# The down projection's low rank products as narrow fp32 matmuls

## The chip, the cores and the metric

One core of one Trainium2 chip runs the whole program. The metric is the device time of one execution in microseconds; for the kernel before it is the median of three runs.

## The reference

Eight samples of 128 tokens, 512 features each. A gated feed forward network whose three projections each have a low rank addition chosen per sample by an index, then a second gated network with an RMS norm, then a residual. Cut to what matters:

```python
def lora_add(base, inp, A, B):
    Ab = A[layer_idx][lora_indices]          # [8, 16, F]: one matrix per sample
    Bb = B[layer_idx][lora_indices]
    t = jnp.einsum('bri,bni->bnr', Ab, inp)
    return base + jnp.einsum('bor,bnr->bno', Bb, t) * SCALE
gate = lora_add(jnp.einsum('bnh,fh->bnf', x, W_gate), x, A_gate, B_gate)
up = lora_add(jnp.einsum('bnh,fh->bnf', x, W_up), x, A_up, B_up)
act = jax.nn.silu(gate) * up
down = lora_add(jnp.einsum('bnf,hf->bnh', act, W_down), act, A_down, B_down)
```

Here F is 1376, the rank 16 and SCALE 0.5. The change concerns the `t` of the last line: for every sample, 16 rows of its own A against its own 128 tokens, summed over F.

## The kernel before, in words

Tokens lie in the free dimension, in two halves t = 0, 1 of 512 tokens (four samples each); features lie on the 128 partitions. F is 11 tiles of 128 (FC), the last one padded. All arithmetic on TensorE aims at fp32 accuracy by splitting: a value is rounded to the type `fp32r` (the hi part, a copy on ScalarE) and what is left is another `fp32r` value (the lo part, a subtraction on VectorE); a product takes three matmuls (`PASSES`: hi x hi, hi x lo, lo x hi). One PSUM bank holds 128 partitions by 512 fp32 values, which is one output tile of one half.

The program is five instruction streams written out by hand, one for each of TensorE (`pe`), VectorE (`v`), ScalarE (`a`), GpSimd (`pool`) and SyncE's DMA queue (`sp`), each in its own fixed order, tied by semaphores. No planner orders anything: the order in the source is the order on the engine.

The work runs in stages. First come the gate and up projections (first a few tiles on their own, then eight groups in a scheme with seven products each, `group(j)`, line 1421), which leave the activations `act` in SBUF as plain fp32. Then the **first down projection**, the stage of the change (lines 1526 to 1635). Its parts on TensorE are:

- `main_c(t, n)` (line 1532, matmuls on line 1528): activation tile n of half t against the weight tile `wdc[n]`, 4 output tiles by 3 passes, 12 matmuls of 512 columns. Its activation comes from a ring of ten slots (`slot_c`), filled by `hi_ac` on ScalarE and `lo_ac` on VectorE; `s_alo` counts filled slots, `s_use` counts used ones. Its weights come by DMA (`load_wd`), are split by `hi_wd` and `lo_wd`, and are counted by `s_wdlo`. A group of 11 for half 0 and of 11 for half 1.
- `t_c(t, n, ...)` (line 1538): the low rank product of this stage. `ad[:, n, t, :]` holds 128 weight columns: 4 samples by 16 of hi, then 4 by 16 of lo. Two matmuls of 512 columns (with the hi and the lo activation slot) give all four samples' A against all four samples' tokens. It runs between the `main_c` calls, since it reads the same slots.
- ScalarE's `td_add` moves the lower 64 rows of the result (the lo part of A) to SBUF; VectorE's `td_sum` adds them to the upper 64 rows and multiplies by a mask that holds 0.5 for the sample's own 16 rows and zero elsewhere; `td_hi` and `td_lo` split the sum into `td`.
- `lora_c(t, h)` (line 1545): B against `td`, two matmuls of 256 columns onto each output tile, which closes it.
- `p4(S1 - 1)` is the last product of the stage before, put between the first two `main_c`. `sum_squares` (line 1552) sums squares of the result over the features for the RMS norm, whose chain (`keep_y`, `square`, `sum_hi`, `rsqrt`, `norm`, `scale`) leads to the next stage's operands.

After the last `lora_c` of half 1 (`close(3)`) the second network begins with `conv` (line 1446).

Of the kernel before, what the change touches and what calls it, by code (L numbers as in the profile page):

```python
# [15 lines left out]
P = 128  # L16
KT = H // P
FC, FF = 11, 14
CH = 512
# [24 lines left out]
def build(nc, xT_in, idx_in, wsh_in, w0_in, wgu_in, wd_in, vs_in, vj_in, agu_in, bgu_in, ad_in, bd_in, lnw_in, out):  # L44
# [4 lines left out]
    with ctx:  # L49
# [21 lines left out]
        with ExitStack() as way:  # L71
            tadd = sb("tadd", [64, CH], f32, way)
            tsum = sb("tsum", [64, CH], f32, way)
            bdr = sb("bdr", [64, 2, H], f32, way)
# [54 lines left out]
        T_BANK = [bank[7], bank[1]]  # L129
# [73 lines left out]
        def unit_act(n):  # L203
# [35 lines left out]
        s_adhi, s_adlo, s_bdhi, s_bdlo = sem("ad_hi"), sem("ad_lo"), sem("bd_hi"), sem("bd_lo")  # L239
        s_ahi, s_alo, s_use = sem("act_hi"), sem("act_lo"), sem("act_used")  # L240
        s_t, s_tadd, s_tsum, s_tmsk, s_tdhi, s_tdlo = (sem(n) for n in (
            "td_projected", "td_added", "td_summed", "td_masked", "td_hi", "td_lo"))
# [131 lines left out]
        @block.gpsimd  # L374
        def _(pool):
            m = mask[0:64, :].rearrange("p (b n) -> p b n", b=4)
            nc.gpsimd.memset(mask[0:64, :], LORA_SCALE).then_inc(s_mask, 1)
            pool.wait_ge(s_mask, 1)
            nc.gpsimd.affine_select(out=m, in_=m, compare_op=ALU.is_ge, fill=0.0, base=0,
                                    pattern=[[-RANK, 4], [0, P]], channel_multiplier=1).then_inc(s_mask, 1)  # L380
            pool.wait_ge(s_mask, 2)
            nc.gpsimd.affine_select(out=m, in_=m, compare_op=ALU.is_ge, fill=0.0, base=RANK - 1,
                                    pattern=[[RANK, 4], [0, P]], channel_multiplier=-1).then_inc(s_mask, 1)
            pool.wait_ge(s_w0hi0, 2)
            nc.gpsimd.memset(act[CR:P, FC - 1, :], 0.0).then_inc(s_act_pad, 1)
            nc.gpsimd.memset(v32(tgu[KS:P, :, :, :]), 0.0).then_inc(s_pad, 1)
            nc.gpsimd.memset(v32(stk0[KS:P, :, :]), 0.0).then_inc(s_pad, 1)
            nc.gpsimd.memset(v32(stk1[KS:P, :, :]), 0.0).then_inc(s_pad, 1)
            nc.gpsimd.memset(v32(tneg[KS:P, :, :]), 0.0).then_inc(s_pad, 1)
            pool.wait_ge(s_p4, S1)  # L390
            for t in range(2):
                nc.gpsimd.memset(v32(bd[t][KS:P, :, :]), 0.0).then_inc(s_pad_d, 1)
                nc.gpsimd.memset(v32(td[t][KS:P, :]), 0.0).then_inc(s_pad_d, 1)

        @block.scalar
        def _(a):
# [200 lines left out]
            def hi_ad():  # L597
                a.wait_ge(s_ad_ld, 16 * B)
                a.wait_ge(s_stklo, 8)
                for b in range(B):  # L600
                    col = RANK * (b % 4)
                    copy(ad[:, :, b // 4, col:col + RANK], ad_raw[:, b, :].rearrange("p (n r) -> p n r", r=RANK)
                         ).then_inc(s_adhi, 1)
# [9 lines left out]
            def td_add(t):  # L613
                a.wait_ge(s_t, t + 1)
                for q in range(2):
                    half = slice(256 * q, 256 * q + 256)
                    copy(tadd[32 * q:32 * q + 32, half], T_BANK[t][64 + 32 * q:96 + 32 * q, half]).then_inc(s_tadd, 1)

            def td_hi(t):
                a.wait_ge(s_tmsk, 2 * t + 2)  # L620
                copy(td[t][0:32, :], tsum[0:32, :]).then_inc(s_tdhi, 1)
                copy(td[t][32:64, :], tsum[0:32, :]).then_inc(s_tdhi, 1)
# [132 lines left out]
            for j in range(S1):  # L755
                group(j, S1)
                if j < 6:
                    stack_hi(j // 2 + 2, j % 2)
                elif j == 6:
                    hi_ad()  # L760
# [10 lines left out]
            td_add(0)  # L771
            td_hi(0)
# [16 lines left out]
            td_add(1)  # L789
            td_hi(1)  # L790
# [55 lines left out]
        def _(v):  # L846
# [163 lines left out]
            def lo_ad():  # L1010
                for b in range(B):
                    col = RANK * (b % 4)
                    v.wait_ge(s_adhi, b + 1)
                    sub(ad[:, :, b // 4, 64 + col:64 + col + RANK], ad_raw[:, b, :].rearrange("p (n r) -> p n r", r=RANK),
                        ad[:, :, b // 4, col:col + RANK]).then_inc(s_adlo, 1)

# [6 lines left out]
            def td_sum(t):  # L1023
                v.wait_ge(s_tadd, 2 * t + 2)
                if t == 1:
                    v.wait_ge(s_tdhi, 2)
                    v.wait_ge(s_tdlo, 1)
                for q in range(2):
                    rows, half = slice(32 * q, 32 * q + 32), slice(256 * q, 256 * q + 256)
                    nc.vector.tensor_tensor(tadd[rows, half], tadd[rows, half], T_BANK[t][rows, half], ALU.add  # L1030
                                            ).then_inc(s_tsum, 1)
                for q in range(2):
                    rows, half = slice(32 * q, 32 * q + 32), slice(256 * q, 256 * q + 256)
                    v.wait_ge(s_tsum, 2 * t + q + 1)
                    nc.vector.tensor_tensor(tsum[0:32, half], tadd[rows, half], mask[rows, half], ALU.mult
                                            ).then_inc(s_tmsk, 1)

            def td_lo(t):
                v.wait_ge(s_tdhi, 2 * t + 1)
                v.wait_ge(s_tmsk, 2 * t + 2)  # L1040
                sub(td[t][64:KS, :], tsum[0:32, :], td[t][0:32, :]).then_inc(s_tdlo, 1)
# [166 lines left out]
            for j in range(S1):  # L1208
                group(j, 0, S1)
                if j == 6:  # L1210
                    lo_ad()
# [14 lines left out]
            td_sum(0)  # L1226
            td_lo(0)
# [17 lines left out]
            td_sum(1)  # L1245
            td_lo(1)
# [84 lines left out]
        def _(pe):  # L1331
# [227 lines left out]
            pe.wait_ge(s_adlo, B)  # L1559
# [19 lines left out]
            pe.wait_ge(s_c21[1], S1 // 2)  # L1579
            pe.wait_ge(s_c12, S1)  # L1580
            pe.wait_ge(s_alo, 12)
            main_c(1, 0, range(3))
            pe.wait_ge(s_tadd, 2)
            pe.wait_ge(s_tsum, 2)
            main_c(1, 0, range(3, 4))
            pe.wait_ge(s_alo, 13)
            main_c(1, 1)
# [4 lines left out]
            pe.wait_ge(s_tdhi, 2)  # L1592
            pe.wait_ge(s_tdlo, 1)
            main_c(0, 10)
            for h in range(4):
                lora_c(0, h).then_inc(s_y, 1)
            pe.wait_ge(s_alo, 14)
            main_c(1, 2).then_inc(s_use, 1)
            pe.wait_ge(s_alo, 15)
            main_c(1, 3)  # L1600
            pe.wait_ge(s_ev, 2)
            t_c(1, 0, True, False).then_inc(s_use, 1)
            for n in range(1, 4):
                t_c(1, n, False, False)
            pe.wait_ge(s_alo, 16)
            main_c(1, 4)
            t_c(1, 4, False, False)
            sum_squares(0, 0)
            for n in range(5, 7):
                pe.wait_ge(s_alo, 11 + n + 1)  # L1610
                main_c(1, n)
                t_c(1, n, False, False)
            for n in range(7, 11):
                pe.wait_ge(s_alo, 11 + n + 1)
                ins = t_c(1, n, False, n == 10)
            ins.then_inc(s_t, 1)
# [12 lines left out]
            pe.wait_ge(s_tdhi, 4)  # L1629
            pe.wait_ge(s_tdlo, 2)  # L1630
# [15 lines left out]
            pe.wait_ge(s_tsum, 4)  # L1646
# [112 lines left out]
```

## Time and profile before

| what | value |
|---|---|
| median of 3 runs | 410.06 us (408.87 to 410.11) |
| the profiled execution's own time | 411.35 us |
| span of its core, first to last instruction | 409.5 us |
| granted TensorE clock, mean | 1.000 |
| instructions | 5437, of them 1849 matmuls |

The span is the profiled part of that execution; its own time is what the runs' times are to be compared with. PE is TensorE's matmul row, PEld its weight load row, DVE is VectorE, ACT is ScalarE, POOL is GpSimd. Matmul records overlap, so that 390 ns of one record don't say how far apart two of them start. Line numbers are those of the kernel before; `L848` and `L398` are helpers (a subtraction on DVE, a copy on ACT), so there the names of the tiles tell which step it is.

### The profile page before, as it was taken

How to read it: one execution, taken by the hardware profiler on the slowest of the kernel's cores; microseconds unless marked ns; L12 is line 12 of the kernel's file. 1: busy time of each engine (PE TensorE's matmuls, PEld its weight loads, DVE VectorE, ACT ScalarE, POOL GpSimd, SP SyncE). 2: the span in 40 equal slices, each digit the busy share in tenths (PEclk: the TensorE clock that was granted, in tenths of full speed). 3: DMA queues.
4: the chain of work that ended last, by engine and by line, in shares of the span. 5: the costliest groups of instructions: out<-in, count | busy, mean ns of one | idle time of the engine just before them, and what ended most of it. 6: DMA issues, size and time to landing. Idle time of an engine off the chain costs nothing.

```text
span 409.5 us, 5437 instructions
## 1 busy us (share of the span) xinstructions
PE 403.8 (99%) x1849; PEld 336.0 (82%) x1849; DVE 314.1 (77%) x483; ACT 239.8 (59%) x377; POOL 12.7 (3%) x16
## 2 busy tenths in 40 slices
PE   8999999999999999999999999999999999999996
PEld 5899888888888888888888888888888888888885
DVE  3779979585856567463889988778787869899993
ACT  4759876757674467731655555555656476384740
POOL 5300000000000200000000000000000000000000
PEclk9999999999999999999999999999999999999999
DMA  7630233311111420300101113131322125205112
GB/s 252 201 113 2 78 108 108 114 51 53 51 53 53 128 78 0 104 0 0 49 4 40 64 52 102 53 102 52 103 84 72 51 90 155 89 1 194 52 51 102
DMA packets 14237, 31.86 MB, mean 78 GB/s; under 512 B 2307, under 2 KB 4611, under 8 KB 14211
## 3 DMA queue, kind: packets, MB, share of 16 engines
q1 hardware_dynamic: 13632, 29.96, 22.6%
q10 hardware_dynamic: 578, 1.57, 1.2%
q8 instruction: 14, 0.23, 0.2%
q14 instruction: 13, 0.10, 0.1%
HBM read 29.43 MB, written 2.10 MB: 77 GB/s over the span
## 4 chain that ended last, share of the span: by engine, by line
PE 97%; DMA 1%; issue 0%; DVE 0%; DVEq 0%; SPq 0%
PE bank L1337 47%; PE bank L1663 16%; PE bank L1528 15%; PE bank L1446 5%; PE bank L1474 3%; PE bank L1493 3%; PE bank L1482 3%; PE bank L1541 2%; PE bank L1347 2%; DMA wraw<-w_in 1%; PE bank L1548 0%; PE bank L1555 0%; DVE act L930 0%; DVEq L49 0%; SPq L289 0%
## 5 line engine op out<-in xcount | busy, mean ns | idle before, releaser
L1337 PE MATMUL bank<-xs,ws 128*128 128x512 f32 x840 | 194.2, 390 | 0.0
L1337 PEld LDWEIGHTS bank<-xs,ws 128*128 128x128 f32 x840 | 156.6, 188 | 32.3 <-ACT bank L398 0.5
L1528 PE MATMUL bank<-xs,wdc 128*128 128x512 f32 x264 | 62.9, 389 | 0.0
L1528 PEld LDWEIGHTS bank<-xs,wdc 128*128 128x128 f32 x264 | 49.3, 188 | 10.1
L398 ACT ACTIVATE xs<-act 128x512 fp32r<-128x512 f32 x71 | 43.0, 625 | 21.1 <-DVE act L995 7.6
L848 DVE TENSOR_TENSOR xs<-act,xs 128x512 fp32r<-128x512 f32 x71 | 47.6, 686 | 4.7 <-ACT xs L398 4.2
L848 DVE TENSOR_TENSOR ws<-wraw,ws 128x256 fp32r<-128x256 f32 (+2 forms) x49 | 32.4, 670 | 14.9 <-ACT ws L398 14.9
L398 ACT ACTIVATE bank<-bank 128x512 f32<-128x512 f32 x30 | 17.4, 580 | 39.5 <-PE bank L1337 38.7
L1663 PE MATMUL bank<-xs,vs 128*128 128x512 f32 x168 | 38.2, 389 | 0.0
L1663 PEld LDWEIGHTS bank<-xs,vs 128*128 128x128 f32 x168 | 31.5, 188 | 6.5
L398 ACT ACTIVATE ws<-wraw 128x256 fp32r<-128x256 f32 (+2 forms) x47 | 28.6, 619 | 12.0 <-PE bank L1337 4.1
L848 DVE TENSOR_TENSOR ws<-wsum,ws 128x1024 fp32r<-128x1024 f32 x20 | 24.5, 1225 | 12.4 <-ACT ws L398 12.4
L398 ACT ACTIVATE mu<-bank 128x512 f32<-128x512 f32 x40 | 23.9, 598 | 17.2 <-PE bank L1337 10.6
L1663 PE MATMUL bank<-xs,ws 128*128 128x512 f32 x126 | 29.0, 389 | 0.0
L1663 PEld LDWEIGHTS bank<-xs,ws 128*128 128x128 f32 x126 | 23.6, 188 | 4.9
L398 ACT ACTIVATE stack<-bgu_raw 32x1024 fp32r<-32x1024 f32 (+1 forms) x20 | 22.8, 1138 | 0.3
L467 ACT ACTIVATE act<-bank 128x512 f32<-128x512 f32 (+1 forms) x30 | 17.4, 593 | 9.4 <-PE bank L1347 8.0
L1446 PE MATMUL bank<-xs,ws 128*128 128x512 f32 x96 | 22.1, 389 | 0.0
L398 ACT ACTIVATE ws<-wsum 128x1024 fp32r<-128x1024 f32 x20 | 21.1, 1053 | 0.8 <-DVE wsum L862 0.8
L1446 PEld LDWEIGHTS bank<-xs,ws 128*128 128x128 f32 x96 | 18.0, 188 | 3.7
L848 DVE TENSOR_TENSOR wdc<-wdr,wdc 128x512 fp32r<-128x512 f32 x11 | 7.6, 688 | 12.6 <-ACT wdc L398 12.6
L848 DVE TENSOR_TENSOR stack<-bgu_raw,stack 32x1024 fp32r<-32x1024 f32 (+1 forms) x10 | 13.2, 1322 | 2.4 <-ACT stack L398 2.2
(124 smaller groups left out, 438.6 us busy)
## 6 DMA issues: line engine op xcount, KB each, us to landing
wraw<-wgu_in SPq DMA_DIRECT2D x22, 512.0 KB, 3.2
wdr<-vs_in SPq DMA_DIRECT2D x7, 512.0 KB, 3.5
wdr<-wd_in SPq DMA_DIRECT2D x11, 256.0 KB, 2.7
wraw<-vj_in SPq DMA_DIRECT2D x3, 896.0 KB, 4.6
xa<-xT_in SPq DMA_DIRECT2D x4, 256.0 KB, 5.0
wraw<-w_in SPq DMA_DIRECT2D x4, 256.0 KB, 5.2
xa<-xT_in ACTq DMA_DIRECT2D x2, 512.0 KB, 5.9
bgu_raw<-bgu_in SPq DMA_DIRECT2D x32, 32.0 KB, 2.0
```

The source lines that it names most:

```text
L398: return nc.scalar.activation(out_ap, in_ap, ACT.Copy, scale=scale)
L467: return nc.scalar.activation(out_ap, in_ap, ACT.Silu, scale=scale)
L848: return nc.vector.tensor_tensor(out_ap, raw, v32(part), ALU.subtract)
L1337: ins = mm(z[:, :], ws[:, j % 2, w, s, k * P:(k + 1) * P], xs[:, c, r, k, :], start=(start and k == 0 and s == 0 and r == 0), stop=(k == 1 ...
L1347: ins = mm(z[0:m, half], stk[c % 2][:, 2 * t + q, cols], t_op[:, half], start=(alone and q == 0), stop=(q == 1), skip_group_check=True)
L1446: ins = mm(z[:, :], ws[:, j % 2, w, s, (k % 2) * P:(k % 2) * P + P], x_op(k, t, r), start=(k == 0 and s == 0 and r == 0), stop=(k == KT - ...
L1474: mm(UNIT_BANK[i][g][:, :], w0_tile(s, k, g, i), x_op(k, 0, r), start=(k == 0 and s == 0 and r == 0), stop=(k == KT - 1 and r == 1), skip_ ...
L1482: mm(UNIT_BANK[n][g][:, :], w0_tile(s, k, g, UNITS[n][0]), x_op(k, 1, r), start=(k == 0 and s == 0 and r == 0), stop=(k == KT - 1 and s == ...
L1493: ins = mm(SHORT_BANK[t][g][:, half], wsh[s][:, k, g, q, :], x_op(k, t, r)[:, half], start=(k == 0 and s == 0 and r == 0 and q == 0), stop ...
L1528: ins = mm(z[:, :], wd[:, s, h * P:(h + 1) * P], x[r], start=(start and s == 0 and r == 0), stop=False, skip_group_check=True)
L1541: ins = mm(T_BANK[t][:, :], ad[:, n, t, :], slot_c(u, r), start=(first and r == 0), stop=(last and r == 1), skip_group_check=True)
L1663: ins = mm(DOWN[p][3][h][:, :], down_w(i, s)[:, h * P:(h + 1) * P], slot_f(i, r), start=(p < 2 and k == 0 and s == 0 and r == 0), stop=(k ...
```

## The change

The low rank products of the first down projection are no longer made of hi and lo parts. `ad` becomes plain fp32, with 48 columns for each pair of samples and each tile n: the even sample's 16, 16 zeros (set by GpSimd), the odd sample's 16. A window of 32 columns is then one sample's A with 16 zeros behind or ahead of it. Each product takes such a window and that sample's 128 tokens of `act`, both plain fp32, and writes 32 partitions of the bank, 32b to 32b + 31 for the sample b of the half: 44 products for a half. Both halves run one after the other, right behind `main_c(0, 3)`, instead of spread over the stage. ScalarE reads the four samples' blocks out of the bank with the factor 0.5 (`td_scale`), which needs neither mask nor addition, and `td_hi` and `td_lo` follow for both halves ahead of the last weight tile. Half 1's bank is bank 6 instead of bank 1. The ring's slots are now free after `main_c`, so `s_use` is counted there, and `main_c(1, n)` runs without a break.

```diff
-            ad = sb("ad", [P, FC, 2, P], f32r, way)
+            ad = sb("ad", [P, B // 2, FC, 3 * RANK], f32, way)
-        T_BANK = [bank[7], bank[1]]
+        T_BANK = [bank[7], bank[6]]
...
             nc.gpsimd.memset(v32(tneg[KS:P, :, :]), 0.0).then_inc(s_pad, 1)
+            pool.wait_ge(s_stklo, 8)
+            nc.gpsimd.memset(ad[:, :, :, RANK:2 * RANK], 0.0).then_inc(s_ad_pad, 1)
+            pool.wait_ge(s_ad_pad, 1)
             pool.wait_ge(s_p4, S1)
...
-            def td_add(t):
+            def td_scale(t):
                 a.wait_ge(s_t, t + 1)
-                for q in range(2):
-                    half = slice(256 * q, 256 * q + 256)
-                    copy(tadd[32 * q:32 * q + 32, half], T_BANK[t][64 + 32 * q:96 + 32 * q, half]).then_inc(s_tadd, 1)
+                for b in range(4):
+                    copy(tsum[:, t, b * P:(b + 1) * P], T_BANK[t][32 * b:32 * b + 32, b * P:(b + 1) * P], LORA_SCALE
+                         ).then_inc(s_tsum, 1)
...
+            for t in range(2):
+                td_scale(t)
+                td_hi(t)
             hi_wd(FC - 1)
             hi_ac(10)
             hi_bd()
             for u in range(11, 18):
                 hi_ac(u)
-            td_add(0)
-            td_hi(0)
             nc.scalar.preload_act_table(ACT.Abs_reciprocal_sqrt)
...
             rsqrt(0)
-            td_add(1)
-            td_hi(1)
...
             for n in range(2, FC - 1):
                 lo_wd(n)
                 lo_ac(n)
+            td_lo(0)
+            td_lo(1)
             lo_wd(FC - 1)
...
             for u in range(11, 18):
                 lo_ac(u)
-            td_sum(0)
-            td_lo(0)
...
             v.wait_ge(s_lnws, 1)
-            td_sum(1)
-            td_lo(1)
...
-            def t_c(t, n, first, last):
-                u = 11 * t + n
-                for r in range(2):
-                    ins = mm(T_BANK[t][:, :], ad[:, n, t, :], slot_c(u, r),
-                             start=(first and r == 0), stop=(last and r == 1), skip_group_check=True)
+            def t_c(t):
+                for n in range(FC):
+                    for b in range(4):
+                        tokens, col = slice(b * P, (b + 1) * P), RANK * (b % 2)
+                        ins = mm(T_BANK[t][32 * b:32 * b + 32, tokens], ad[:, 2 * t + b // 2, n, col:col + 2 * RANK],
+                                 act_at(ORDER_C[n], t)[:, tokens], start=(n == 0), stop=(n == FC - 1), skip_group_check=True)
                 return ins
...
-            pe.wait_ge(s_adlo, B)
...
+                main_c(0, n).then_inc(s_use, 1)
                 if n == 0:
-                    main_c(0, 0)
                     p4(S1 - 1)
-                    pe.wait_ge(s_b22, S1)
-                    t_c(0, 0, True, False).then_inc(s_use, 1)
-                elif n < 9:
-                    main_c(0, n)
-                    t_c(0, n, False, False).then_inc(s_use, 1)
-                else:
-                    t_c(0, 9, False, False)
-                    pe.wait_ge(s_alo, 11)
-                    t_c(0, 10, False, True).then_inc(s_t, 1)
-                    main_c(0, 9).then_inc(s_use, 1)
...
+                if n == 3:
+                    pe.wait_ge(s_ad, B)
+                    pe.wait_ge(s_ad_pad, 1)
+                    pe.wait_ge(s_cl, S1)
+                    pe.wait_ge(s_shm, 2)
+                    pe.wait_ge(s_act_pad, 1)
+                    pe.wait_ge(s_um, 4)
+                    pe.wait_ge(s_c21[1], S1 // 2)
+                    t_c(0).then_inc(s_t, 1)
+                    pe.wait_ge(s_c12, S1)
+                    pe.wait_ge(s_c12f, S1 // 2)
+                    pe.wait_ge(s_c22f, S1 // 2)
+                    t_c(1).then_inc(s_t, 1)
+            pe.wait_ge(s_alo, 11)
             pe.wait_ge(s_wdlo, FC)
+            main_c(0, 10).then_inc(s_use, 1)
...
+            pe.wait_ge(s_tdhi, 4)
+            pe.wait_ge(s_tdlo, 2)
             for h in range(4):
                 lora_c(0, h).then_inc(s_y, 1)
...
+            pe.wait_ge(s_tsum, 8)
+            for n in range(7):
                 pe.wait_ge(s_alo, 11 + n + 1)
-                main_c(1, n)
-                t_c(1, n, False, False)
...
+                ins = main_c(1, n)
+                if n == 0:
+                    ins.then_inc(s_use, 1)
+                elif n == 3:
+                    sum_squares(0, 0)
+            pe.wait_ge(s_alo, 22)
```

`lo_ad`, `td_sum`, `tadd` and the 128 column form of `ad` are gone; `hi_ad` becomes `place_ad`, which makes the same eight copies into the new form.

## Rows read from the trace of the kernel before

**Rows 1.** The page's busy line of TensorE and its chain of waits, by engine.
```profile
PE 403.8 (99%) x1849; PEld 336.0 (82%) x1849; DVE 314.1 (77%) x483; ACT 239.8 (59%) x377; POOL 12.7 (3%) x16
...
PE 97%; DMA 1%; issue 0%; DVE 0%; DVEq 0%; SPq 0%
```

**Rows 2.** The stretches view: stretch, its length, each engine's busy us, PEclk, DMA.
```profile
core 0: us, PE busy (x) PEld busy (x) DVE busy (x) ACT busy (x) POOL busy (x), PEclk, DMA share, GB/s
...
128.03:201.97 73.94, 73.94 (x336) 61.46 (x334) 45.23 (x72) 38.73 (x65) 2.79 (x4) 1.00 0.15 47
```

**Rows 3.** The chain in order of time, 126 to 206 us: start us, us, what.
```profile
132.51 0.47 PE bank L1541 x2
...
135.71 0.45 PE bank L1541 x2
136.16 2.72 PE bank L1528 x12
...
157.92 1.36 PE bank L1541 x6
...
170.16 0.95 PE bank L1548 x8
...
176.58 1.81 PE bank L1541 x8
...
181.12 0.46 PE bank L1541 x2
...
184.82 0.45 PE bank L1541 x2
...
188.00 2.27 PE bank L1541 x10
```

**Rows 4.** TensorE's groups by line, 128.03 to 201.97 us: count, busy us, mean ns.
```profile
L1541 PE MATMUL bank<-xs,ad 128*128 128x512 f32 x44 | 12.1, 390 | 0.0
L1548 PE MATMUL bank<-ws 128*128 128x256 f32 x16 | 2.7, 281 | 0.0
```

**Rows 5.** TensorE's matmuls and weight loads in order of time, around one t_c.
```profile
138.27 0.62 PE L1528 MATMUL bank<-xs,wdc 128*128 128x512 f32 x2
138.50 0.41 PEld L1541 LDWEIGHTS bank<-xs,ad 128*128 128x128 f32 x2
138.72 0.61 PE L1541 MATMUL bank<-xs,ad 128*128 128x512 f32 x2
138.95 2.68 PEld L1528 LDWEIGHTS bank<-xs,wdc 128*128 128x128 f32 x12
```

**Rows 6.** VectorE, then GpSimd, in order of time: start us, us, what, idle before.
```profile
132.55 0.69 DVE L914 SCALAR_TENSOR_TENSOR act<-bank,act 128x512 f32<-128x512 f32 x1 [1.57 <-PE bank L1347]
...
133.76 0.68 DVE L848 TENSOR_TENSOR xs<-act,xs 128x512 fp32r<-128x512 f32 x1
...
177.86 0.69 DVE L848 TENSOR_TENSOR xs<-sqr,xs 128x512 fp32r<-128x512 f32 x1 [0.70 <-ACT xs L398]
...
132.57 0.95 POOL L392 MEMSET ws<- 32x1024 f32 x1 [118.44 <-PE bank L1347]
133.47 0.52 POOL L393 MEMSET ws<- 32x512 f32 x1
```

**Rows 7.** ScalarE in order of time, then two of its groups by line.
```profile
150.35 0.64 ACT L398 ACTIVATE wdc<-wdr 128x512 fp32r<-128x512 f32 x1
...
159.52 0.78 ACT L398 ACTIVATE tadd<-bank 32x256 f32<-32x256 f32 x2
162.39 1.29 ACT L398 ACTIVATE ws<-tsum 32x512 fp32r<-32x512 f32 x2 [2.09 <-DVE tsum L1035]
...
166.05 2.18 ACT L398 ACTIVATE ws<-wraw 128x768 fp32r<-128x768 f32 x4
170.43 2.07 ACT L398 ACTIVATE nx<-bank 128x512 f32<-128x512 f32 x4 [2.21 <-PE bank L1548]
...
L398 ACT ACTIVATE ws<-tsum 32x512 fp32r<-32x512 f32 x4 | 2.5, 632 | 4.1 <-DVE tsum L1035 4.0
...
L398 ACT ACTIVATE tadd<-bank 32x256 f32<-32x256 f32 x4 | 1.5, 379 | 7.6 <-PE bank L1541 7.5
```

More of the change, by code:

```diff
@@ L71, in build @@
         with ExitStack() as way:
-            tadd = sb("tadd", [64, CH], f32, way)
-            tsum = sb("tsum", [64, CH], f32, way)
+            tsum = sb("tsum", [32, 2, CH], f32, way)
             bdr = sb("bdr", [64, 2, H], f32, way)
@@ L238, in build @@
         s_wdhi, s_wdlo = sem("wd_hi"), sem("wd_lo")
-        s_adhi, s_adlo, s_bdhi, s_bdlo = sem("ad_hi"), sem("ad_lo"), sem("bd_hi"), sem("bd_lo")
+        s_ad, s_ad_pad, s_bdhi, s_bdlo = sem("ad_placed"), sem("ad_padding_zero"), sem("bd_hi"), sem("bd_lo")
         s_ahi, s_alo, s_use = sem("act_hi"), sem("act_lo"), sem("act_used")
-        s_t, s_tadd, s_tsum, s_tmsk, s_tdhi, s_tdlo = (sem(n) for n in (
-            "td_projected", "td_added", "td_summed", "td_masked", "td_hi", "td_lo"))
+        s_t, s_tsum, s_tdhi, s_tdlo = (sem(n) for n in ("td_projected", "td_scaled", "td_hi", "td_lo"))
         s_y, s_sq, s_sqd, s_acc, s_sqhi, s_sqlo, s_ev, s_nm = (sem(n) for n in (
@@ L595, in copy_u2, with place_ad @@
                     copy(du2[:, i, :], DB_BANK[i][:, :]).then_inc(s_dcu, 1)
-            def hi_ad():
+            def place_ad():
                 a.wait_ge(s_ad_ld, 16 * B)
@@ L600, in hi_ad @@
                 for b in range(B):
-                    col = RANK * (b % 4)
-                    copy(ad[:, :, b // 4, col:col + RANK], ad_raw[:, b, :].rearrange("p (n r) -> p n r", r=RANK)
-                         ).then_inc(s_adhi, 1)
+                    col = 2 * RANK * (b % 2)
+                    copy(ad[:, b // 2, :, col:col + RANK], ad_raw[:, b, :].rearrange("p (n r) -> p n r", r=RANK)
+                         ).then_inc(s_ad, 1)
             def hi_bd():
@@ L611, in hi_bd @@
                     copy(bd[t][64:KS, :, :], raw).then_inc(s_bdhi, 1)
-            def td_add(t):
+            def td_scale(t):
                 a.wait_ge(s_t, t + 1)
-                for q in range(2):
-                    half = slice(256 * q, 256 * q + 256)
-                    copy(tadd[32 * q:32 * q + 32, half], T_BANK[t][64 + 32 * q:96 + 32 * q, half]).then_inc(s_tadd, 1)
+                for b in range(4):
+                    copy(tsum[:, t, b * P:(b + 1) * P], T_BANK[t][32 * b:32 * b + 32, b * P:(b + 1) * P], LORA_SCALE
+                         ).then_inc(s_tsum, 1)
             def td_hi(t):
-                a.wait_ge(s_tmsk, 2 * t + 2)
-                copy(td[t][0:32, :], tsum[0:32, :]).then_inc(s_tdhi, 1)
-                copy(td[t][32:64, :], tsum[0:32, :]).then_inc(s_tdhi, 1)
+                a.wait_ge(s_tsum, 4 * t + 4)
+                copy(td[t][0:32, :], tsum[:, t, :]).then_inc(s_tdhi, 1)
+                copy(td[t][32:64, :], tsum[:, t, :]).then_inc(s_tdhi, 1)
             def keep_y(m):
@@ L759, in _ @@
                 elif j == 6:
-                    hi_ad()
+                    place_ad()
             for n in range(FC - 1):
@@ L1008, in lo_ac @@
                 sub(slot_c(u, 1), act_at(ORDER_C[n], t), slot_c(u, 0)).then_inc(s_alo, 1)
[L1010 to L1015, printed above, removed]
             def lo_bd():
@@ L1021, in lo_bd @@
                         ).then_inc(s_bdlo, 1)
[L1023 to L1036, printed above, removed]
             def td_lo(t):
                 v.wait_ge(s_tdhi, 2 * t + 1)
-                v.wait_ge(s_tmsk, 2 * t + 2)
-                sub(td[t][64:KS, :], tsum[0:32, :], td[t][0:32, :]).then_inc(s_tdlo, 1)
+                v.wait_ge(s_tsum, 4 * t + 4)
+                sub(td[t][64:KS, :], tsum[:, t, :], td[t][0:32, :]).then_inc(s_tdlo, 1)
             def add_square(t, h):
@@ L1209, in _ @@
                 group(j, 0, S1)
-                if j == 6:
-                    lo_ad()
             c22_sum(S1 - 1)
@@ L1565, in _ @@
                 pe.wait_ge(s_wdlo, n + 1)
+                main_c(0, n).then_inc(s_use, 1)
                 if n == 0:
-                    main_c(0, 0)
                     p4(S1 - 1)
-                    pe.wait_ge(s_b22, S1)
-                    t_c(0, 0, True, False).then_inc(s_use, 1)
-                elif n < 9:
-                    main_c(0, n)
-                    t_c(0, n, False, False).then_inc(s_use, 1)
-                else:
-                    t_c(0, 9, False, False)
-                    pe.wait_ge(s_alo, 11)
-                    t_c(0, 10, False, True).then_inc(s_t, 1)
-                    main_c(0, 9).then_inc(s_use, 1)
[L1579 to L1587, printed above, removed]
+                if n == 3:
[12 more added lines that the diff above has]
+            pe.wait_ge(s_alo, 11)
             pe.wait_ge(s_wdlo, FC)
+            main_c(0, 10).then_inc(s_use, 1)
             pe.wait_ge(s_bdhi, 4)
@@ L1591, in _ @@
             pe.wait_ge(s_pad_d, 4)
-            pe.wait_ge(s_tdhi, 2)
-            pe.wait_ge(s_tdlo, 1)
-            main_c(0, 10)
+            pe.wait_ge(s_tdhi, 4)
+            pe.wait_ge(s_tdlo, 2)
             for h in range(4):
                 lora_c(0, h).then_inc(s_y, 1)
[L1597 to L1603, printed above, removed]
-                t_c(1, n, False, False)
[L1605 to L1609, printed above, removed]
-                pe.wait_ge(s_alo, 11 + n + 1)
-                main_c(1, n)
[L1612 to L1616, printed above, removed]
+            pe.wait_ge(s_tsum, 8)
+            for n in range(7):
+                pe.wait_ge(s_alo, 11 + n + 1)
+                ins = main_c(1, n)
[4 more added lines that the diff above has]
+            pe.wait_ge(s_alo, 22)
             def rest(h):
@@ L1628, in _ @@
             rest(2)
-            pe.wait_ge(s_tdhi, 4)
-            pe.wait_ge(s_tdlo, 2)
             close(0)
```

1 line of the change is left out of this document (removed).

## The prediction

> **What bounds the kernel now.** I read the page's busy line first, then its chain of waits, then the stretches, then the chain in order of time. TensorE is busy 99% of the span with 1,849 matmuls, and 97% of the chain that ends last is TensorE itself [rows 1]. In the stretch that the change rewrites, 128.03 to 201.97 us, it never rests: 73.94 of 73.94 us busy at a granted clock of 1.00, which is the 2.4 GHz level, while VectorE is busy 45.23 and ScalarE 38.73 us [rows 2]. So a matmul taken out is worth its own step, and VectorE or ScalarE work taken out is worth nothing unless TensorE waits for it. The step is read from the chain in order of time: twelve matmuls of 512 columns take 2.72 us, 0.2267 us each; eight of 256 columns take 0.95 us, 0.119 us each [rows 3]. A single record lasts 390 ns or 281 ns [rows 4]; it overlaps the next, so the chain's step is the price.
>
> **What is removed.** t_c had 44 matmuls of 512 columns [rows 4]. In the chain they stand as one pair of 0.47 us, seven of 0.45 us, runs of 1.36, 1.81 and 2.27 us, and pairs of 0.46 and 0.45 us [rows 3]: 0.47 + 3.15 + 1.36 + 1.81 + 0.46 + 0.45 + 2.27 = 9.97 us, all on the path. The rest of line 1528's matmuls, p4, lora_c and sum_squares stay, in another order.
>
> VectorE loses lo_ad and td_sum, ScalarE td_add, and PE the waits for them. I price these at 0: TensorE did not wait for any of them [rows 2].
>
> **What is added on TensorE.** 88 products of 32 weight columns by 128 tokens, plain fp32, in two runs of 44 after the fourth main_c. No row shows an fp32 product or one narrower than 128 weight columns, so both ends come from the nearest rows. The two steps lie on a line, (0.2267 - 0.119) / 256 per column, which puts 128 columns at about 0.065 us, an estimate. Cheapest: one pass each and four at a time, 22 x 0.065 = 1.4 us. Dearest: an fp32 value is, in this kernel, a rounded part and a remainder; their products make four combinations, so 4 x 128 = 512 columns, the 0.2267 us row, and each product alone in its turn: 88 x 0.2267 = 19.9 us. Between them lies four combinations with four products at a time: 22 x 0.2267 = 5.0 us. I take 5.0. For the width: the steps of 512 and 256 columns follow the columns that stream, though each has a full load of 128 weight columns of its own; that load is hidden, since the 188 ns load of the next matmul starts while the one before is in flight [rows 5]. For four at a time: the four samples of a group write four different quarters of the bank's partitions, so they need no common columns of the array. Nothing in the trace shows the array used so; that is the open point, and the rivals are made of it. Entering and leaving the narrow shape may cost one emptying of the array each: 0.390 - 0.227 = 0.16 us, twice, 0.3 us.
>
> The Trainium skill, TensorEngine Tiling (Array Packing), Key Properties, says that column tiles run independently and that a change of the tiling mode drains TensorE; no run here shows either. The Trainium skill, FP8 and Floating Point Precision, TensorE Precision Notes, gives true FP32 four passes; the Trainium skill, Perfetto Trace Analysis, Engine Utilization, only halves the output rate for FP32_LOW_HIGH, by which the sum would have 2.6 us in place of 5.0.
>
> **What is moved, and what might wait.** Without t_c the PE clock reads: main_c(0,1) begins at 132.5, main_c(0,3) ends at 140.7, the two runs end at 146.0 (with 5.3 us), main_c(0,9) ends at 162.3, lora_c at 166.0, the fourth main_c of the second half at 176.8.
> - Weights and activations of the first groups: the remainder of slot 2 is done at 134.4 [rows 6]; PE now needs it at 135.2 instead of 136.2 [rows 3]. The margin shrinks to 0.8 us and grows again by the length of the runs. Nothing.
> - The runs' inputs: the last activation is multiplied at 132.55 to 133.24 [rows 6], 7 us before 140.7. POOL's memset of ad (704 values a partition, between the 0.5 us of 512 values and the 0.95 us of 1,024) lies in a stretch where POOL is idle for 118 us [rows 6]; its later memsets wait for p4 as before, so nothing queued behind it is late. DVE's next waits are for weights. The moved PE waits cost nothing.
> - ScalarE now has td_scale and td_hi for both halves ahead of hi_wd(10), which starts at 150.35 before [rows 7]. Eight copies of 32x128 are at most eight of the 379 ns copies of 32x256 [rows 7], say 0.29 us; with four of 632 ns [rows 7] this is 4.9 us, in place of the 4.17 us (with its wait) from 159.52 to 163.69 [rows 7]. Everything up to keep_y is thereby 0.7 us late: hi_wd(10) at 155.3, hi_bd done at 160.7, bd's remainder some 1.2 us later. PE wants slot 10 at 162.3 and bd at 165.0: covered. lo_wd(10) on DVE waits with it; SP's next loads wait for later work than that.
> - keep_y started at 170.43, right after lora_c. ScalarE is now free for it at 169.0 (end of hi_b at 168.23 [rows 7], plus 0.7), 3 us after lora_c's end; it becomes the late one. The square's remainder came 8.1 us after keep_y's start (178.55 [rows 6]), so at 177.1; sum_squares(0, 0) is reached at 176.8. A wait of 0.3 us. Beyond it, norm(0) no longer queues behind td_sum(1) on DVE and scale is some 9 us early: nothing.
> - Behind close(3) the order and the waits are those of before; SP and POOL have no issue moved past another.
>
> **Sum.** -9.97 + 5.0 + 0.3 + 0.3 = -4.4 us, on a span of 409.5 us. The profiled execution took 411.35 us in all, 1.3 us above the median of 410.06, so the same difference on the median gives **405.7 us**, 1.1% faster. A measurement of this kernel can tell about 0.3%, 1.2 us, from no change.
>
> **Rivals.**
> 1. *Products in turn* (slower). The four quarters do not run together, or the array is held as one whatever the output's partitions say, so the change doesn't do what its shape promises. Price: 88 x 0.2267 = 19.9 us in place of 5.0, no wait at sum_squares: -9.97 + 19.9 + 0.3 = +10.2, so 420.3 us. It decides from 44 steps on: above 44 x 0.2267 = 9.97 us the runs cost more than what they replace. For it: no row shows two matmuls of this kernel sharing the array. Against it: loads and matmuls here do overlap [rows 5]. The Trainium skill, TensorE: Matmul & The Clock Gate, Part 3, has a rule that speaks for it: a load runs beside a matmul in flight only where the row groups differ, and these four share all 128 rows. By that rule the four would go one by one; the trace disagrees for the full array, where loads into the same rows start before the last matmul is done (188 ns loads within 227 ns steps) [rows 5].
> 2. *Half side by side* (same or slightly slower). An fp32 product goes as two records, one for the weights' rounded part and one for the remainder, each streaming 256 columns at 0.119 us. Both use the same quarter, and the records of this trace start in program order, so the second waits for the first, and only it overlaps the next product's first: 88 x 0.119 = 10.5 us, with 0.3 us 10.8, so +0.8: 410.9 us. With four records of 128 columns three of them are exposed: 88 x 3 x 0.065 = 17.2 us, +7.5: 417.6. For it: the kernel's own split needs two weight loads. Against it: an f32r product is one load and one matmul (1,849 of each) [rows 1].
> 3. *The wait takes it back.* If ScalarE's copies from the bank cost the full 379 ns and DVE's chain adds to that, sum_squares waits 1.5 us rather than 0.3: 406.9 us. It stays on the faster side, within my case.
>
> **How the numbers follow.** My case 0.46 (rival 3 is in it), half side by side 0.32, in turn 0.22. Faster by over 0.3%: my case and a sliver of rival 2, 0.47. Within 0.3%: rival 2 with two records and few extras, 0.13. Slower: the rest of rival 2 and all of rival 1, 0.40. My case's own range is 403.5 to 407.5: down if a product streams only as much as 256 columns (22 x 0.119 = 2.6 in place of 5.0), up for the wait and for groups that take 0.3 us. The whole range, 403.5 to 417.5, takes in rival 2 and leaves out rival 1. The bound of 1.4 us (402.1) has no reason of its own and is left out too.
>
> **What would show it.** In the profile after: two runs of line t_c near 140.7 us that last about 5 us together, four starts close to one another and then a gap of some 0.22 us; main_c(0,4) at about 146; sum_squares(0, 0) within 0.5 us of its turn; close(3) near 197.5 instead of 201.9, and all later work shifted by the same 4.4 us. Records twice or four times 88, evenly spaced, mean rival 2; even starts 0.2 us apart mean rival 1. A granted clock below 1.00 in the runs' stretch would make any of these prices too low, and the prediction wrong on the slow side.

## The result and the profile after

The changed kernel takes 405.18 us in the median of 4 runs (404.01 to 406.00), the kernel before, on the same chips, 409.47 us (408.69 to 410.11). The ratio is 0.9882, with a 95% interval from 0.9855 to 0.9910: 1.2% faster, where 1.1% and 405.7 us were forecast. The profiled execution took 405.77 us with a span of 403.9 us.

The page of the changed kernel, its busy line and its chain of waits by engine (they answer to [rows 1]):

```profile
PE 398.2 (99%) x1981; PEld 332.0 (82%) x1981; DVE 309.1 (77%) x467; ACT 240.5 (60%) x381; POOL 13.4 (3%) x17
...
PE 97%; DMA 1%; issue 0%; DVE 0%; DVEq 0%; SPq 0%
```

TensorE still sets the end, and it is as busy as before. With one matmul record for each of the 88 products it would have 88 - 44 = 44 records more; it has 1981 - 1849 = 132 = 176 - 44. So each of the 88 fp32 products is two matmul records on the chip, each with a weight load of its own. The stage's chain in order of time, 126 to 206 us (answers to [rows 3]; L1502 is main_c, L1516 t_c, L1523 lora_c, L1530 sum_squares, L1420 conv):

```profile
127.64 2.72 PE bank L1502 x12
130.36 1.36 PE bank L1311 x6
131.72 0.23 PE bank L1321 x2
131.95 8.19 PE bank L1502 x36
140.13 4.94 PE bank L1516 x176
145.08 19.31 PE bank L1502 x84
164.38 0.95 PE bank L1523 x8
165.34 10.91 PE bank L1502 x48
176.25 0.48 PE bank L1530 x2
176.73 15.01 PE bank L1502 x66
...
196.57 0.23 PE bank L1523 x2
196.80 2.07 PE bank L1420 x9
```

This is one unbroken row of TensorE work, with the run of narrow products as a single piece of 4.94 us. The same two ends in the kernel before, where L1528 is main_c and L1446 conv:

```profile
128.20 2.72 PE bank L1528 x12
...
202.13 2.07 PE bank L1446 x9
```

From the first main_c to the first conv it is 196.80 - 127.64 = 69.16 us, where the kernel before took 202.13 - 128.20 = 73.93 us: 4.77 us less. That covers the whole change of the median (4.3 us) and most of that between the two profiled spans (409.5 to 403.9, 5.6 us). The other 0.8 us lies where the code of TensorE is the same: 0.56 us ahead of the stage, 0.27 us behind it. In the kernels below main_c(0,0) starts anywhere between 125.7 and 127.9 us, so this part is a difference of executions, not of the change.

TensorE's groups by line in that stretch, and the narrow loads (answers to [rows 4]):

```profile
L1516 PE MATMUL bank<-act,ad 128*32 128x128 f32 x176 | 5.0, 273 | 0.0
...
L1516 PEld LDWEIGHTS bank<-act,ad 128*32 128x32 f32 x176 | 4.7, 110 | 0.4 <-issue 0.4
```

A record of 273 ns every 4.94 / 176 = 28 ns: by the modelled ends, some ten are in flight at a time. What the groups hide are the starts. Taken from the trace's records, they come four at a time; the numbers are nanoseconds from one start to the next, at the run's start and in its middle, with the wide matmuls' own step (227) ahead:

```
wide, wide, then the run:  227 227 318   7   6   7 113   7   7   6  90   6   7   7  89 ...
middle of the run:         ...  89   6   7   7  89   7   6   7  89 ...
the run's end, then wide:  ...  89   7   7   6 203 341 240 235
```

Four records start within 20 ns, then 89 ns pass: 109.5 ns for four. 44 such groups are 4.82 us. Going in costs 318 - 227 = 91 ns, coming out 203 - 89 = 114 ns at the first wide start and 341 - 227 = 114 ns at the second, 0.32 us in all for the way in and out.

### The profile page after: what moved, and what is told of

The parts are those of the page before. It is cut to its first block, busy times and chain, and to the rows that moved or that the text cites. A ratio compares the mean times of both kernels' runs of the same rounds, so it can differ in the third digit from the quotient of the medians.

```text
span 403.9 us, 5691 instructions
## 1 busy us (share of the span) xinstructions
PE 398.2 (99%) x1981; PEld 332.0 (82%) x1981; DVE 309.1 (77%) x467; ACT 240.5 (60%) x381; POOL 13.4 (3%) x17
## 4 chain that ended last, share of the span: by engine, by line
PE 97%; DMA 1%; issue 0%; DVE 0%; DVEq 0%; SPq 0%
PE bank L1311 47%; PE bank L1618 17%; PE bank L1502 15%; PE bank L1420 5%; PE bank L1448 3%; PE bank L1467 3%; PE bank L1456 3%; PE bank L1321 2%; PE bank L1516 1%; DMA wraw<-w_in 1%; PE bank L1523 0%; PE bank L1530 0%; DVE act L930 0%; DVEq L49 0%; SPq L287 0%
## 5 line engine op out<-in xcount | busy, mean ns | idle before, releaser
L1502 PE MATMUL bank<-xs,wdc 128*128 128x512 f32 x264 | 61.5, 390 | 0.0
L1502 PEld LDWEIGHTS bank<-xs,wdc 128*128 128x128 f32 x264 | 49.1, 188 | 10.2 <-DVE xs L848 0.2
L1420 PE MATMUL bank<-xs,ws 128*128 128x512 f32 x96 | 22.1, 389 | 0.0
L399 ACT ACTIVATE ws<-wsum 128x1024 fp32r<-128x1024 f32 x20 | 21.1, 1054 | 0.8 <-DVE wsum L862 0.8
L1420 PEld LDWEIGHTS bank<-xs,ws 128*128 128x128 f32 x96 | 18.0, 188 | 3.7
```

Of the source, the lines that this page charges most:

```text
L399: return nc.scalar.activation(out_ap, in_ap, ACT.Copy, scale=scale)
L1420: ins = mm(z[:, :], ws[:, j % 2, w, s, (k % 2) * P:(k % 2) * P + P], x_op(k, t, r), start=(k == 0 and s == 0 and r == 0), stop=(k == KT - ...
L1502: ins = mm(z[:, :], wd[:, s, h * P:(h + 1) * P], x[r], start=(start and s == 0 and r == 0), stop=False, skip_group_check=True)
```

## The experiments

Nine kernels, all made from the changed one. Each alters either t_c's loops or the place of the run; what the low rank product computes is the reference's, except where the expectation says otherwise. The times are medians; the ratio to the kernel before comes from runs of both on the same chip. The kernel before had 409.4 to 411.0 us in these series.

**1. The samples in turn.**

```diff
-                for n in range(FC):
-                    for b in range(4):
+                for b in range(4):
+                    for n in range(FC):
```

> The same 88 products, but all eleven tiles of one sample before the next sample, so that neighbours use the same quarter of the array. Theory SIDE (what the four quarters do at the same time is what makes the run short, and one record of 128 fp32 columns streams for about 0.1095 us): 176 records one behind the other, 176 x 0.1095 = 19.3 us in place of 4.94, some 14.3 us more than the changed kernel's 405.2, so 419.5 us. Rival RECORD (a narrow record is cheap whichever quarter it uses, 28 ns each, because its weight load is short): the run stays at 4.9 us and the time at 405.2 us.

Measured: 415.43 us, ratio 1.0119 (1.0080 to 1.0157), 10.2 us above the changed kernel's median. The same 176 records, in the chain of this kernel:

```profile
138.54 16.49 PE bank L1516 x176
155.03 19.27 PE bank L1502 x84
```

RECORD falls: the same records with the same loads take 16.49 us in place of 4.94 when neighbours share a quarter. So what the changed kernel lives on is the four quarters streaming together. SIDE is right in kind, and its run is 2.8 us too long: within one sample the records do start 109 ns apart, but at each border between samples the starts read

```
109 109 110   5 104  30  79  30  79  30 109 109
```

Two rows of starts, 109 ns apart each, run through one another for some four records. No record names its quarter; two rows at the pace of one quarter each are read as the next sample's records starting while the last ones of the sample before still wait for theirs. Seven borders save 2.8 us, 0.4 us or 3.6 records each. So TensorE does not start narrow records strictly in program order, and the description ahead of the prediction, by which the order in the source is the order on the engine, does not hold for them.

**2. Two samples in alternation.**

```diff
-                for n in range(FC):
-                    for b in range(4):
+                for pair in range(2):
+                    for n, b in [(n, 2 * pair + i) for n in range(FC) for i in range(2)]:
```

> The same 88 products, two samples in alternation, then the other two. SIDE: two quarters at a time, 88 x 0.1095 = 9.6 us in place of 4.94, 4.7 us more: 409.9 us, the time of the kernel before. RECORD: 4.9 us, 405.2 us.

Measured: 408.30 us, ratio 0.9961 (0.9936 to 0.9985), and in the chain of this kernel

```profile
140.36 8.53 PE bank L1516 x176
```

With two quarters at a time the run takes 8.53 us. The 1.1 us that lack to the expected 9.6 are three borders of the kind above. SIDE holds.

**3. Half the columns.**

```diff
-                        tokens, col = slice(b * P, (b + 1) * P), RANK * (b % 2)
+                        tokens, col = slice(b * P, b * P + 64), RANK * (b % 2)
```

> Each product streams only the first 64 of its sample's 128 tokens; the other 64 are left out of the low rank product. SIDE, with the columns streamed as the price: 44 groups of four at 0.053 + 0.003 us = 2.5 us, 2.4 us less than the changed kernel: 402.8 us. RECORD, with weight loads or the issue of records as the price: 176 x 28 ns as before, 4.9 us, 405.2 us.

Measured: 404.88 us, ratio 0.9874 (0.9826 to 0.9923): not told apart from the changed kernel. By the median RECORD would win, but the chain of this kernel says otherwise:

```profile
138.31 2.58 PE bank L1516 x172
140.89 2.26 issue
143.15 0.30 PE bank L1516 x4
```

172 of the 176 records pass in 2.58 us, in groups of four that are 56 ns apart: 53 ns of streaming and 3 ns, as SIDE has it. Then TensorE stands for 2.26 us, put down to "issue", with no semaphore behind it, and the last four follow. The gain was made and lost within the run. Experiment 9 takes that gap up.

**4. Eight runs instead of one stretch.** Two or three groups of four products stand behind every three matmuls of main_c(0,4) and (0,5).

```diff
-                main_c(0, n).then_inc(s_use, 1)
+                if n in (4, 5):
+                    for h in range(4):
+                        ins = main_c(0, n, range(h, h + 1))
+                        for tile in range(3 * h, min(3 * h + 3, FC)):
+                            last = t_c(n - 4, range(tile, tile + 1))
+                        if h == 3:
+                            last.then_inc(s_t, 1)
+                else:
+                    ins = main_c(0, n)
+                ins.then_inc(s_use, 1)
...
-                    t_c(0).then_inc(s_t, 1)
...
-                    t_c(1).then_inc(s_t, 1)
```

> The same products in the same order, but in eight runs of eight or twelve, each behind three wide matmuls of the fifth and sixth weight tile, instead of in one unbroken stretch. If going in and out of the narrow shape empties the array (0.32 us for a run by the gaps in the trace of the changed kernel): 7 x 0.32 = 2.2 us more, 407.4 us. If the gaps belong to the run's start alone (weights to be fetched, first records): 405.2 us. ScalarE's reads come some 2 us later in either case, and sum_squares may wait up to 0.5 us.

Measured: 407.09 us, ratio 0.9914 (0.9887 to 0.9941), 1.9 us above the changed kernel. Its chain:

```profile
140.74 0.79 PE bank L1516 x24
141.53 0.89 PE bank L1502 x3
142.43 0.79 PE bank L1516 x24
```

24 records should take 6 x 0.1095 = 0.66 us and take 0.79; three wide matmuls should take 0.68 and take 0.89. Each round trip between the shapes costs 0.13 + 0.21 = 0.34 us. Seven more of them are 2.4 us, and from the first main_c to the first conv this kernel takes 199.14 - 127.56 = 71.58 us, 2.42 us more than the changed kernel; sum_squares does not wait. That agrees with the emptying of 0.16 us each way that the prediction worked out. It is what the changed kernel saves by placing both runs together: with no other shape between them, they pay it once.

**5. Plain fp32 without the narrow shape.**

```diff
+                wide = ad[:, 2 * t:2 * t + 2, :, :].rearrange("p q n c -> p (q n c)")
                 for n in range(FC):
-                    for b in range(4):
-                        tokens, col = slice(b * P, (b + 1) * P), RANK * (b % 2)
-                        ins = mm(T_BANK[t][32 * b:32 * b + 32, tokens], ad[:, 2 * t + b // 2, n, col:col + 2 * RANK],
-                                 act_at(ORDER_C[n], t)[:, tokens], start=(n == 0), stop=(n == FC - 1), skip_group_check=True)
+                    ins = mm(T_BANK[t][:, :], wide[:, 32 * n:32 * n + P],
+                             act_at(ORDER_C[n], t), start=(n == 0), stop=(n == FC - 1), skip_group_check=True)
```

> Plain fp32 without the narrow shape: 22 products of 128 weight columns by all 512 tokens in the place of the 88. As weights each reads 128 neighbouring columns of the narrow form, so the low rank term that is added is another one than the reference's. The narrow run showed two records for each fp32 product, and 0.1095 us of streaming for one record of 128 columns. Theory FOUR (each of the two records streams every column twice): 22 x 2 x 0.43 = 18.9 us in place of 4.94, 14 us more than the changed kernel's 405.2: 419 us. Rival TWO (a wide fp32 product streams its columns twice in all): 9.4 us, 409.7 us.

Measured: 418.23 us, ratio 1.0225 (1.0208 to 1.0242). Its records and its chain:

```profile
L1515 PE MATMUL bank<-act,ad x44: 590/592/592, 138.1 to 156.5; 128*128 128x512 f32 x44
```

```profile
138.24 18.88 PE bank L1515 x44
```

FOUR holds: 44 records in 18.88 us, 429 ns each, which is twice the 213 ns that 512 columns take at 2.4 GHz, and 3 ns. With two records a product that makes four passes. The Trainium skill, FP8 and Floating Point Precision, TensorE Precision Notes, gives four; the trace agrees. The halved rate that the Trainium skill, Perfetto Trace Analysis, Engine Utilization, gives for FP32_LOW_HIGH fits one record here; a sum by it alone is short by a factor of two, since a product is two records. Plain fp32 on the full array makes the kernel 2.2% slower: the type alone does not give the gain, the narrow shape is needed. The other half of that question, rounded parts in the narrow shape, was not run.

**6. Two tiles deep.**

```diff
-                for n in range(FC):
-                    for b in range(4):
+                for first in range(0, FC, 2):
+                    for b, n in [(b, n) for b in range(4) for n in range(first, min(first + 2, FC))]:
```

> The same 88 products with two tiles of one sample ahead of the next sample, so that four records of one quarter stand in a row in the program. Theory REACH (TensorE starts a record ahead of older ones whose quarter is busy, but only some four records ahead, as the borders between samples in the kernel with the samples in turn suggest): about two quarters at a time, 7 to 10 us in place of 4.94: 407.5 to 410 us. Rival FAR (it looks as far ahead as it needs): 5 us, 405.2 us. Rival ORDER (records start strictly in program order): three of four records of a quarter exposed, 88 x 3 / 4 x 2 x 0.1095 = 14.5 us, 414.7 us.

Measured: 404.64 us, ratio 0.9897 (0.9878 to 0.9915), and in the chain of this kernel

```profile
138.39 5.15 PE bank L1516 x176
```

ORDER falls, and REACH, as I had put it, falls too: with four records of a quarter in a row all four quarters still stream together. Twelve older records stood ahead of the fourth quarter's first one. A reach counted over the whole program can't be both about four (experiment 1) and above twelve. One counted for each quarter can, which made the next theory.

**7. The run five groups later.**

```diff
-                if n == 3:
+                if n == 8:
                     pe.wait_ge(s_ad, B)
```

> The two runs stand behind the ninth main_c of the first half instead of the fourth; nothing else changes. If only TensorE's own work counts: 405.2 us. By the theory that the run's place is covered by ScalarE only while its result is there when ScalarE comes to it (148.0 us in the changed kernel's trace): the results come at 153.3 and 155.7 us, ScalarE is then some 5 us late down to keep_y and the squares, the eleventh main_c waits 1 us for its slot and sum_squares(0, 0) some 3 us more: 408 to 410 us.

Measured: 414.02 us, ratio 1.0122 (1.0102 to 1.0141): 8.8 us above the changed kernel, more than the 3 to 5 that I worked out. The run itself takes 4.95 us (151.91 to 156.86 us). TensorE's waits in this kernel, 150 to 200 us, where the changed kernel has none:

```profile
PE bank L1530 <- DVE xs L848: 3.9, 1, 3.9
PE bank L1502 <- DVE xs L848: 1.7, 1, 1.7
PE bank L1523 <- ACT ws L399: 0.6, 1, 0.6
```

ScalarE stood 8.12 us for the products:

```profile
154.59 1.15 ACT L399 ACTIVATE tsum<-bank 32x128 f32<-32x128 f32 x4 [8.12 <-PE bank L1516]
```

It had all that it has to do for main_c(0,10), lora_c and the squares queued behind that. The places are those of the expectation (slot, then bd, then sum_squares); the sizes add up to 6.2 us. More came from the clock. The chain of this kernel behind the last wait, then its stretches around it (engine busy columns as in [rows 2]):

```profile
181.44 0.93 PE bank L1530 x2
182.37 16.40 PE bank L1502 x66
...
177.40:181.40 4.00, 0.18 (x1) 0.00 (x0) 2.70 (x5) 2.72 (x5) 0.00 (x0) 1.00 0.18 72
181.40:184.40 3.00, 2.96 (x8) 2.37 (x9) 2.90 (x7) 0.69 (x1) 0.00 (x0) 0.57 0.00 0
184.40:190.00 5.60, 5.60 (x25) 4.55 (x24) 5.50 (x8) 1.90 (x2) 0.00 (x0) 0.93 0.00 0
```

After TensorE had rested for 3.9 us, the granted clock fell to a mean of 0.57 for 3 us, most of the time at its lower level (1.2 GHz), and the 66 matmuls that take 15.01 us in the changed kernel took 16.40. The remaining 1.2 us I put down to the matmuls next to each wait, which overlap none on that side (sum_squares' two take 0.93 us in place of 0.48); that sum is not shown piece by piece.

**8. Four tiles deep.** As experiment 6 with 4 in the place of 2.

```diff
-                for n in range(FC):
-                    for b in range(4):
+                for first in range(0, FC, 4):
+                    for b, n in [(b, n) for b in range(4) for n in range(first, min(first + 4, FC))]:
```

> The same 88 products with four tiles of one sample ahead of the next sample: eight records of one quarter in a row. Theory QUEUE (records are handed out in program order, and each quarter holds about four of them, running one included; a full quarter holds up all that come behind): worked through with 0.1095 us a record and four places this gives 9.3 us, in place of 4.94 (the same working gives 16.2 for the samples in turn, 8.4 for the pairs and 4.9 for two deep, measured 16.5, 8.5 and 5.15): some 409.5 us. With three places 11.8 us, 412 us. Rival FAR (no bound that matters): 5 us, 405 us.

Measured: 409.84 us, ratio 0.9988 (0.9963 to 1.0013), and in the chain of this kernel

```profile
140.39 9.98 PE bank L1516 x176
```

QUEUE's four places gave 9.3 us, three 11.8, FAR 5. The run took 9.98, as long as the 44 matmuls that the change removed, and the time is that of the kernel before. Four places for each quarter thus give all five orders to within 0.7 us: 4.8, 4.9, 8.4, 9.3, 16.2 worked through against 4.94, 5.15, 8.53, 9.98, 16.49. Only the 9.3 was worked out ahead of its run; the other four were known when the theory was made. "About four places" is what the runs support; nothing in them shows a queue as such.

**9. Half the columns, the two runs apart.** As experiment 3, with the second half's run one main_c later.

```diff
                     t_c(0).then_inc(s_t, 1)
+                if n == 4:
                     pe.wait_ge(s_c12, S1)
```

> As with 64 tokens a product (the other 64 left out), but the second half's run stands one main_c later than the first half's. Theory SUPPLY (the gap of 2.26 us in the run of 64 columns is TensorE out of instructions, since the run takes 352 records in 2.6 us): 2.7 us of wide matmuls between let the supply catch up, the gap goes or shrinks below 1 us, at the price of one more entry of 0.3 us: 403.0 us. Rival FIXED (something else holds the run's end): a gap of 2 us stays: 405 us.

Measured: 404.17 us, ratio 0.9859 (0.9820 to 0.9897). TensorE in order of time in this kernel:

```profile
139.06 1.44 PE L1516 MATMUL bank<-act,ad 128*32 128x64 f32 x88
140.43 3.03 PE L1502 MATMUL bank<-xs,wdc 128*128 128x512 f32 x12
143.39 1.44 PE L1516 MATMUL bank<-act,ad 128*32 128x64 f32 x88
144.76 15.50 PE L1502 MATMUL bank<-xs,wdc 128*128 128x512 f32 x67
```

The gap is gone: each run of 88 records takes 1.4 us without a break. That speaks for SUPPLY, and against anything tied to the end of the products. The time did not follow all the way, since sum_squares now waits for the squares:

```profile
PE bank L1530 <- DVE xs L848: 0.9, 1, 0.9
```

So 404.2 stands where 403.0 was expected, and against 404.9 of experiment 3 the difference is no more than the executions scatter.

The traces' DMA records fit SUPPLY too. In experiment 3 one packet of 16 KB on an instruction queue runs from 140.34 to 141.67 us: it is still under way when the stop begins (140.89 us), and the last four records follow 1.5 us behind it. In the changed kernel the packet of this place (141.84 to 142.72 us) is through 2 us before the run's last four records start, in experiment 9 (140.83 to 141.71 us) nearly 3 us. No row says which engine that queue feeds, so that instructions ran out in experiment 3 remains an inference, from where the stop lies, from what removes it and from this packet.

## Why the prediction was right

**What bounds the kernel.** Right. In experiments 1, 2, 5, 6 and 8 only the order or shape inside the run differs, TensorE shows no wait in the stage, and the time follows the run's length: 1 + (run - 9.97) / 410 gives 1.016, 0.996, 1.022, 0.988 and 1.000 for measured 1.0119, 0.9961, 1.0225, 0.9897 and 0.9988. All but the first lie in the measured intervals, and that one lies just above its upper end (1.0157).

**What is removed, 9.97 us.** Experiment 8 confirms it by substitution: a run of 9.98 us gives the old time back, with lo_ad, td_sum and td_add still taken out. So that work was worth nothing measurable, as priced, though VectorE's busy time between the first main_c and the first conv fell from 45.06 to 42.03 us.

**What is added, 5.0 us.** 4.82 us measured. The mechanism was right, four passes and four products at a time: a group of four takes 2 x 0.1095 = 0.219 us, where 0.2267 was taken. The form was not foreseen. Each product is two records of 0.1095 us, not one of 0.2267, so four starts are followed by a gap of 0.09 us and not of 0.22. I had taken pairs of records for the mark of the half-overlapped rival, at 10.5 us or more, since the second would hold up all that follows. The pairs were there, in groups of four rather than evenly spaced, and held up nothing: the step that failed inside that rival is "start in program order". A cost near its price came only where eight records of one quarter stand in a row (experiment 8, 9.98 us).

**Going in and out, 0.3 us.** 0.32 us in the starts of the changed kernel, 0.34 us a round trip in experiment 4. The Trainium skill, TensorEngine Tiling (Array Packing), Key Properties, says that a change of mode drains TensorE and that the tiles run independently; this case agrees with both, with the second only as long as no more than about four records of a tile stand in a row.

**The wait at sum_squares, 0.3 us.** It did not come. ScalarE in order of time in the changed kernel (answers to [rows 7]), then VectorE's last step for the squares:

```profile
146.90 0.63 ACT L399 ACTIVATE wdc<-wdr 128x512 fp32r<-128x512 f32 x1
...
147.96 1.13 ACT L399 ACTIVATE tsum<-bank 32x128 f32<-32x128 f32 x4
149.13 1.29 ACT L399 ACTIVATE ws<-tsum 32x512 fp32r<-32x512 f32 x2
150.44 1.15 ACT L399 ACTIVATE tsum<-bank 32x128 f32<-32x128 f32 x4
151.62 1.29 ACT L399 ACTIVATE ws<-tsum 32x512 fp32r<-32x512 f32 x2
152.93 0.63 ACT L399 ACTIVATE wdc<-wdr 128x512 fp32r<-128x512 f32 x1
...
166.65 2.07 ACT L399 ACTIVATE nx<-bank 128x512 f32<-128x512 f32 x4
...
174.07 0.69 DVE L848 TENSOR_TENSOR xs<-sqr,xs 128x512 fp32r<-128x512 f32 x1 [0.70 <-ACT xs L399]
```

The inserted work takes 152.93 - 147.96 = 4.97 us, where 4.9 was worked out. But it begins at 148.0 us, not 150.35: ScalarE is held up by the weights' landings. hi_wd(9), the weight copy shortly ahead of it, starts at 146.90 us here; in the trace of the kernel before it stood until 149.26 us for its weights:

```profile
149.26 0.63 ACT L398 ACTIVATE wdc<-wdr 128x512 fp32r<-128x512 f32 x1 [1.74 <-DMA wdr<-wd_in]
```

Counted from the first main_c, hi_wd(9) starts after 21.1 us there, after 19.3 us in the changed kernel and after 19.4 to 19.8 us in the nine experiments. By the landings in the traces that load took 4.4 us in the one profiled execution before and 2.5 to 3.0 us in all the others, so the forecast took one late landing for the rule. keep_y starts at 166.65 in place of 169.0, and sum_squares at 176.25 finds its operand, done at 174.76 us: a margin of 1.5 us. With the late landing it would have been a wait of some 0.3 us, an estimate. How thin the margin is, experiments 7 and 9 show: results that came late (7), or TensorE at sum_squares 2 us sooner (9), turned into waits.

**Rivals.** In turn: its shape was made in experiment 1, and takes 16.5 us rather than 19.9, mostly for the borders' overlap. The rule that stood for it, that a load runs beside a matmul in flight only with other row groups (the Trainium skill, TensorE: Matmul & The Clock Gate, Part 3), would have given such a run; the trace disagrees in the narrow shape too, where four loads on the same 128 rows start 7 ns apart, beside matmuls in flight.

**The sum.** -9.97 + 4.82 + 0.32 = -4.83 us; the stage lost 4.77 us, the median 4.3, and -4.4 was forecast. The terms of the forecast hold to 0.2 us but for the wait. That the median agrees with it to 0.1 us is chance: the four runs of the changed kernel lie 2.0 us apart. One bound does not follow from its own term: 2.6 in place of 5.0 takes 405.7 to 403.3 us, not to 403.5; nothing hangs on it here.

## What to carry to other kernels

Where a product needs few output partitions, plain fp32 in quarters of the array can beat a split into rounded parts on the full array: here 88 products cost 4.9 us where 44 full matmuls cost 10.0, while plain fp32 on the full array cost 18.9. Whether rounded parts in the quarters would be faster still was not run. Write the quarters in rotation, with no more than two products of one quarter in a row, and keep all narrow work in one unbroken stretch, since each way into the narrow shape and back costs 0.3 us here. Put the stretch early enough that the engine that reads its result never has to wait: with both runs five groups later the kernel took 8.8 us longer, twice the gain.

## What was not expected of the hardware

- A plain fp32 product is two records with a weight load each; a record streams each column twice (109 ns for 128 columns, 429 ns for 512).
- By the starts at the borders of experiment 1, TensorE starts narrow records ahead of older ones whose quarter is busy. Orders with 2, 4, 8 and 22 records of a quarter in a row took 4.94, 5.15, 9.98 and 16.49 us, which about four places for each quarter give to within 0.7 us.
- A run of 176 records with 64 columns stopped for 2.26 us near its end with no semaphore behind it, while a packet on an instruction queue was under way; in two runs with 12 wide matmuls between there was no such stop.
- In experiment 7 the granted clock stayed at 1.00 through rests of TensorE of 1.7 and 0.6 us; after a third one of 3.9 us it fell to a mean of 0.57 for 3 us.
